# Router scores spread through memory, and the order of the loop's side stages changed, in a cross-attention and routed-FFN kernel

## The reference

```python
x = x + xattn(layernorm(x), ctx, mask)          # 16 heads of 16, 1024 keys, masked keys by column
x = x + routed_ffn(layernorm(x))
# routed_ffn, per batch of 512 rows y:
scores = y @ w_router
idx = top_k(scores, 128)                        # ordered by score, ties by position
x_sel = y[idx]; h = rmsnorm(x_sel, g1)
x_attn = causal_attention(h) @ W_out.T          # 128 rows, 16 heads
h2 = rmsnorm(x_sel + x_attn, g2)
x_ff = silu(h2 @ W1.T) * (h2 @ W2.T) @ W3.T
out = y.at[idx].set(x_sel + x_attn + x_ff)
```

## Time and profile before

| | |
|---|---|
| time, median of 3 runs | 895.89 us (893.83 to 895.96) |
| time of the profiled execution | 896.05 us |
| its span | 894.3 us |
| TensorE busy | 852.3 us, 95% of the span |
| ScalarE busy | 569.8 us, 64% |
| VectorE busy | 313.4 us, 35% |
| GpSimd busy | 123.5 us, 14% |
| mean granted TensorE clock | 0.993 of full speed |

### The profile page before, as it was taken

How to read it: one execution, slowest core, us unless ns; L and a number is a source line. 1 busy time by engine, 2 the same in 40 slices (tenths; PEclk the granted TensorE clock), 3 DMA queues, 4 the chain that set the end, 5 groups by cost and what they waited for, 6 DMA issues and landing times. The chain is left out here.

```text
span 894.3 us, 28250 instructions
## 1 busy us (share of the span) xinstructions
PE 852.3 (95%) x11779; PEld 294.9 (33%) x11785; DVE 313.4 (35%) x918; ACT 569.8 (64%) x644; POOL 123.5 (14%) x175
## 2 busy tenths in 40 slices
PE   7999999999999999999999999999999999989774
PEld 2322232324323332334323333234323342224343
DVE  3132135421552226421553316422354214411631
ACT  3566767676677767666577766676576766776110
POOL 4000102020120102120120101101121100210110
PEclk9999999999999999999999999999999999999898
DMA  5060201210011200111011200102001100200000
GB/s 183 17 227 1 78 3 31 55 58 24 7 37 49 79 8 27 59 32 49 9 37 49 79 8 25 45 20 78 7 10 53 31 8 2 61 1 4 7 25 9
DMA packets 27577, 35.56 MB, mean 40 GB/s; under 512 B 2083, under 2 KB 24142, under 8 KB 27448
## 3 DMA queue, kind: packets, MB, share of 16 engines
q1 hardware_dynamic: 24952, 31.73, 11.2%
q0 software_dynamic: 2496, 1.98, 1.4%
HBM read 27.53 MB, written 8.93 MB: 41 GB/s over the span
## 5 line engine op out<-in xcount | busy, mean ns | idle before, releaser
L511 ACT ACTIVATE probs<-pair_bank 128x1024 f32<-128x1024 f32 x512 | 496.3, 1021 | 225.4 <-ACTq L510 225.4
L481 PE MATMUL pair_bank<-q_sb,k_sb 32*64 32x512 f32 x4096 | 286.4, 612 | 10.0 <-PEq L478 9.6
L500 PE MATMUL o_bank<-probs,va 128*32 128x512 f32 x2048 | 273.3, 604 | 1.3 <-ACT probs L511 1.1
L500 PEld LDWEIGHTS o_bank<-probs,va 128*32 128x32 f32 x2048 | 41.5, 108 | 205.4 <-issue 114.2
L481 PEld LDWEIGHTS pair_bank<-q_sb,k_sb 32*64 32x64 f32 x4096 | 60.9, 129 | 145.0 <-issue 145.0
L266 PE MATMUL m_bank<-wv_sb,ctx_in 128*32 128x256 f32 x1024 | 61.5, 380 | 0.0
L266 PE MATMUL m_bank<-ctx_in,wk_sb 128*32 128x512 f32 x480 | 60.3, 592 | 0.0
L628 DVE TENSOR_SCALAR va<-m_bank,valid 128x256 f32<-128x256 f32 x64 | 28.1, 480 | 91.6 <-DVEq L625 91.6
L586 DVE STREAM_TRANSPOSE o_blk<-o_bank 128x512 f32<-128x512 f32 x32 | 22.9, 717 | 92.7 <-DVEq L585 92.7
L266 PEld LDWEIGHTS m_bank<-hid_t,w 128*32 128x32 f32 x1392 | 39.5, 110 | 17.0 <-issue 16.0
L266 PEld LDWEIGHTS m_bank<-wv_sb,ctx_in 128*32 128x32 f32 x1024 | 33.5, 110 | 34.2 <-issue 18.9
(11 more groups left out here) (173 smaller groups left out, 604.1 us busy)
## 6 DMA issues: line engine op xcount, KB each, us to landing
ctx_in<-in_ctxT SPq DMA_DIRECT2D x7, 1024.0 KB, 5.0
x_in<-in_x SPq DMA_DIRECT2D x8, 512.0 KB, 4.0
x<-in_x SPq DMA_DIRECT2D x8, 512.0 KB, 4.3
mask_in<-in_mask SPq DMA_DIRECT2D x8, 512.0 KB, 3.9
out_dram<-base SPq DMA_DIRECT2D x8, 512.0 KB, 5.5
ctx_in<-in_ctxT SPq DMA_DIRECT2D x2, 512.0 KB, 7.5
mask_row<-in_mask SPq DMA_DIRECT2D x8, 128.0 KB, 3.9
x_tok<-in_order SPq DMA_DIRECT2D x7, 128.5 KB, 2.0
```

The lines of the kernel that those rows point to most:

```text
L481: last = nc.tensor.matmul(pair_bank[pairs[r // 2]][j:j + 64, r % 2], key_tile(b, s, r)[:, j:j + 64], query_tile(b, s, r), start=True, stop ...
L500: last = nc.tensor.matmul(o_bank[32 * r:32 * r + 32], va[b % 2][:, t, HV * h:HV * h + 32], probs[s % 2][:, r], start=(t == 0), stop=(t == ...
L511: nc.scalar.activation(probs[s % 2][:, 2 * e:2 * e + 2, :], pair_bank[p][:], ACT.Exp, scale=HD ** -0.5).then_inc(s_free[p], 1)
```

## The change

Stage spread is gone from TensorE and ScalarE. SyncE now stores the scores to a DRAM row of 512 numbers, waits for that, and loads the row back to all 128 partitions. The row has the scores of rows 4p to 4p+3 of the (p t) layout side by side, so VectorE's order stages read it with a step of four numbers (16 bytes) where they read consecutive ones before; the second operand and the output are read and written as before. `pe_scores` waits for each pair of banks right before the two heads that go into it. In the loop's tables V0 moves from step 3 to step 0 (on VectorE it moves ahead of wo0), K00 as a whole becomes a stage of the batch two ahead, in steps 30 and 31, V1 is done in halves in steps 5 and 6 (on VectorE behind xn and ahead of order0), K01 moves up to steps 11 and 12 and Q1 down to 17 and 18, hidT and what follows it are one step earlier, and norm1 on VectorE stands behind k. Batch 0 does every P stage in halves over steps 8 to 29. The part "a"/"b" of `dve_norm` is not used by the tables.

```diff
-FS_STEP = 17
-PE_SLOT = [("P", "K00:1", 0, False), ("F", "wo0", 1, False), ("F", "wo1", 2, False), ("P", "V0", 3, True),
-           ("P", "K11:0", 4, False), ("P", "K11:1", 5, False), ("F", "spread", 6, False), ("P", "xT0", 7, False), ("P", "xT1", 8, False),
-           ("P", "Q0:0", 9, False), ("P", "Q0:1", 10, False), ("P", "V1", 11, False), ("P", "Q1:0", 12, False), ("P", "Q1:1", 13, False),
-           ("F", "hidT", 14, False), ("F", "q", 15, False), ("F", "k", 16, False), ("F", "v", FS_STEP, False),
...
-           ("F", "down:0", 29, False), ("F", "down:1", 30, False), ("X", "K00:0", 31, False)]
+FS_STEP = 16
+PE_SLOT = [("P", "V0", 0, False), ("F", "wo0", 1, False), ("F", "wo1", 2, False), ("P", "K11:0", 3, False), ("P", "K11:1", 4, False),
+           ("P", "V1:0", 5, False), ("P", "V1:1", 6, False), ("P", "xT0", 7, False), ("P", "xT1", 8, False), ("P", "Q0:0", 9, False),
+           ("P", "Q0:1", 10, False), ("P", "K01:0", 11, False), ("P", "K01:1", 12, False), ("F", "hidT", 13, False), ("F", "q", 14, False),
+           ("F", "k", 15, False), ("F", "v", FS_STEP, False), ("F", "fs", FS_STEP, False), ("P", "V2", FS_STEP, False),
+           ("P", "Q1:0", 17, False), ("P", "Q1:1", 18, False), ("F", "pv", 19, False), ("P", "V3", 20, False), ("F", "wout", 21, False),
...
+           ("F", "w1", 27, False), ("F", "down:0", 28, False), ("F", "down:1", 29, False), ("X", "K00:0", 30, False), ("X", "K00:1", 31, False)]
...
-DVE_ORDER = [("A", "norm3"), ("F", "wo0"), ("F", "wo1"), ("P", "V0"), ("F", "y"), ("P", "stats"), ("P", "xn"), ("F", "order0"),
-             ("F", "order1"), ("N", "norm0"), ("F", "order2"), ("F", "order3"), ("P", "Q0"), ("P", "V1"), ("F", "selected"), ("P", "Q1"),
-             ("F", "base"), ("F", "q"), ("N", "norm1"), ("F", "k"), ("P", "V2"), ("F", "pv"), ("P", "V3"), ("F", "wout"),
+DVE_ORDER = [("A", "norm3"), ("P", "V0"), ("F", "wo0"), ("F", "wo1"), ("F", "y"), ("P", "stats"), ("P", "xn"), ("P", "V1"), ("F", "order0"),
+             ("F", "order1"), ("N", "norm0"), ("F", "order2"), ("F", "order3"), ("P", "Q0"), ("F", "selected"), ("F", "base"),
+             ("F", "q"), ("F", "k"), ("N", "norm1"), ("P", "V2"), ("P", "Q1"), ("F", "pv"), ("P", "V3"), ("F", "wout"),
...
+        def spread_scores(sp):
+            sp.wait_ge(score_ready, 1)
+            sp.sem_inc(score_ready, -1)
+            sp.dma_start(score_row.rearrange("(p t) -> p t", t=QT), score[:]).then_inc(score_stored, 16)
+            sp.wait_ge(score_stored, 16)
+            sp.sem_inc(score_stored, -16)
+            sp.dma_start(all_scores[:], score_row.partition_broadcast(P)).then_inc(spread_in, 16)
...
             pairs = [ring(b, s, e) for e in range(2)]
-            for p in pairs:
-                pe.wait_ge(s_free[p], 1)
-                pe.sem_inc(s_free[p], -1)
             for r in range(HG):
+                if r % 2 == 0:
+                    pe.wait_ge(s_free[pairs[r // 2]], 1)
+                    pe.sem_inc(s_free[pairs[r // 2]], -1)
...
+                by_tile = lambda a: a.rearrange("p (t q) -> p t q", t=QT)
+                if note is put:
+                    others = all_scores[:].rearrange("p (q t) -> p t q", t=QT)
...
-                nc.vector.scalar_tensor_tensor(out=ties[0][:, ahead], in0=others[:, ahead], scalar=score[:, t:t + 1],
-                                               in1=before[:, t, ahead], op0=ALU.is_ge, op1=ALU.mult,
+                nc.vector.scalar_tensor_tensor(out=by_tile(ties[0][:])[:, ahead], in0=others[:, ahead], scalar=score[:, t:t + 1],
+                                               in1=by_tile(before[:, t])[:, ahead], op0=ALU.is_ge, op1=ALU.mult,
...
                 for b in range(B):
+                    if b > 0:
+                        spread_scores(sp)
                     if b + 2 < B:
                         load_x(sp, b + 2)
```

More of the change, by code:

```diff
@@ L67 @@
+ACT_SLOT = [("P", "K11", 4), ("P", "xT0", 7), ("P", "xT1", 8), ("P", "K01", 12), ("F", "hidT", 13), ("F", "v", FS_STEP),
+            ("F", "fs", FS_STEP), ("P", "differ", 20), ("P", "K10", 22), ("F", "hid2T", 23), ("F", "u0", 24), ("F", "u1", 26), ("X", "K00", 31)]
+DVE_ORDER = [("A", "norm3"), ("P", "V0"), ("F", "wo0"), ("F", "wo1"), ("F", "y"), ("P", "stats"), ("P", "xn"), ("P", "V1"), ("F", "order0"),
[2 rows of a table added]
              ("N", "norm2"), ("F", "u0"), ("F", "w0"), ("F", "u1"), ("F", "w1"), ("F", "down")]
@@ L69 @@
 PE_SLOT_0 = [("I", "V0", 0, False), ("I", "V1", 1, False), ("I", "K10", 2, False),
[4 rows of a table removed]
[L74 to L77, removed]
[7 rows of a table added]
@@ L78 @@
+ACT_SLOT_0 = [("I", "K10", 2), ("I", "K11", 4), ("P", "K00", 9), ("P", "K01", 11), ("P", "K10", 13), ("P", "K11", 15),
+              ("P", "xT0", 18), ("P", "differ", 20), ("P", "xT1", 21), ("X", "K00", 31)]
+DVE_ORDER_0 = [("I", "V0"), ("I", "V1"), ("I", "V2"), ("I", "V3"), ("I", "Q1"), ("P", "stats"), ("N", "norm0"), ("P", "xn"),
+               ("N", "norm1"), ("P", "V0"), ("P", "V1"), ("P", "V2"), ("N", "norm2"), ("P", "Q0"), ("P", "V3"), ("P", "Q1")]
 POOL_ORDER = [("F", "var"), ("P", "var"), ("F", "scatter"), ("F", "rms0"), ("F", "causal"), ("F", "rms1"), ("P", "differ"), ("F", "add")]
@@ L298, in pe_project @@
                 n = int(stage[1])
-                dst = take_bank(pe, i)
-                for e in range(2):
+                dst = bank[i] if part == 1 else take_bank(pe, i)
+                for e in share(part, 2):
                     t = 2 * n + e
@@ L303, in pe_project @@
                                    [(ctx_in[:, c, t * P:(t + 1) * P], wv[:, c, :]) for c in range(KC)])
-                last.then_inc(done["V"], 1)
+                if part != 0:
+                    last.then_inc(done["V"], 1)
             elif stage[0:2] == "xT":
@@ L713, in dve_ffn @@
                 note = put if stage[0:5] == "order" else select
[L715 to L725 removed]
+                by_tile = lambda a: a.rearrange("p (t q) -> p t q", t=QT)
+                if note is put:
+                    others = all_scores[:].rearrange("p (q t) -> p t q", t=QT)
+                    if t == 0:
+                        dve.wait_ge(spread_in, 16)
+                        dve.sem_inc(spread_in, -16)
+                elif i == MISC:
+                    others = by_tile(all_scores[:])
+                    if t == 0:
+                        dve.wait_ge(all_ready, 1)
+                        dve.sem_inc(all_ready, -1)
+                else:
+                    others = by_tile(bank[i])
+                    if t == 0:
+                        dve.wait_ge(done["spread"], 1)
+                        dve.sem_inc(done["spread"], -1)
+                ahead, behind = slice(0, t + 1), slice(t, QT)
+                nc.vector.scalar_tensor_tensor(out=by_tile(ties[0][:])[:, ahead], in0=others[:, ahead], scalar=score[:, t:t + 1],
+                                               in1=by_tile(before[:, t])[:, ahead], op0=ALU.is_ge, op1=ALU.mult,
                                                accum_out=rank[:, t, 0:1])
[L727 to L728 removed]
+                nc.vector.scalar_tensor_tensor(out=by_tile(ties[1][:])[:, behind], in0=others[:, behind], scalar=score[:, t:t + 1],
+                                               in1=by_tile(before[:, t])[:, behind], op0=ALU.is_gt, op1=ALU.is_gt,
                                                accum_out=rank[:, t, 1:2])
```

31 lines of the change are left out of this document (11 added, 20 removed), and 14 rows, old and new, of tables (PE_SLOT, PE_SLOT_0).

## The result

The changed kernel took 900.76 us in the median of 20 runs (896.77 to 903.44), the kernel before, beside it, 895.92 (893.38 to 898.64). The ratio is 1.005, 95% interval 1.0036 to 1.0064: 4.8 us slower, where + 5.6 was predicted. Its profiled execution took 897.49 us, near the low end of its own runs, with a span of 895.7.

What follows compares the result with a forecast made beforehand. TensorE, hardly ever idle in the loop, was taken to bound the kernel; - 3.9 - 3.5 - 3.4 + 4.9 + 0.9 + 7.2 + 3.4 = + 5.6 us gave 901.5 us, range 890.5 to 905.5.

Steps and rivals of the forecast that it cites:

- the likeliest case: The penalty of stepped reads on VectorE holds and hidT waits: 901.5 us, own range 897.5 to 906, chance 0.60.
- Batch 0: Of batch 0's 12 empty steps 11 get half a stage, each saving 0.36 us of waiting: 3.9 us less.
- Stage v: Step 17, batches 1 to 6: v's wait for a bank goes with k ahead of norm1 on VectorE, 3.4 us less.
- wo0 behind V0: Batches 1 to 6: wo0 waits for the bank VectorE's V0 frees behind norm3, 0.81 us each, 4.9 us more.
- xT0 behind V1: Batches 1 to 6: xT0 waits for the bank VectorE's V1 frees behind xn, 0.15 us each, 0.9 us more.
- The way of the scores: Store and load through memory take 5.0 us, bounds 4.2 and 8; order0 in batches 1 to 6 isn't delayed up to 6.6.
- Rival 3: The scores' round trip through memory is late, 8 us or more: 899.9 us, with the penalty near 911; chance 0.05.
- The step of 16 bytes: VectorE's order stages take 1.84 instead of 1.04 ns an element, making hidT wait 1.2 us a batch: 7.2 us more.
- Rival 2: Stepped reads cost VectorE nothing, hidT keeps its slot: 892.4 us, faster; chance 0.31.
- Batch 7: No side work covers the chain: hidT 1.6 us later, one more step behind it 2.1, less 0.3: 3.4 us more.
- Waits apart: Separate waits for the scores' bank pairs: worth 0.3 us behind hidT in batch 7, nothing in busy steps.
- Rival 4: Waiting apart breaks the scores up, a 0.05 us gap in each of 256 steps: 914 us, chance 0.02.

Runs made afterwards that it cites:

- the repeat: Both kernels run once more unchanged: before 895.46 us, changed kernel 898.74 us, ratio to before 1.0044, with profiled executions close to their medians.
- the first pair: The first measurement of both kernels with their profiled executions: changed kernel 900.76 us, kernel before 895.92 us, ratio 1.005.
- scores in tiles: Changed kernel plus a ScalarE copy that puts the transferred scores into tile order, so VectorE counts from unit steps: 900.33 us, ratio to before 1.0051.
- the new order without the transfers: Changed kernel, but scores spread as before by four transposes and a ScalarE copy, V1 whole in step 6: 894.7 us, ratio to before 0.9985.
- transfers alone: Kernel before with the scores spread by the two transfers and read with a step, stage spread removed, old order kept: 898.04 us, ratio 1.0027.

## Why the prediction was right

The direction, the size and the likeliest case held: + 5.6 predicted, + 4.8 and, in the repeat, + 3.3 measured. The mechanism is the predicted one: the stepped counts make hidT late in a slot without slack. But one of the prediction's own signs of being wrong did show: TensorE stood in two places that its list doesn't have, in step 12 of batch 0 and for 2.45 us at step 9 of batch 7. By its steps:

- **Batch 0**, - 3.9: measured - 2.3 and - 2.6 with K00:1 taken out. The steps are 2.90 us as said; the stall of 1.4 to 1.7 in step 12 is what is missing, and nothing in the trace of before told of it.
- **Spread**, - 3.5: held. Step 6 with its transposes (2.62) and V1 whole (3.77) became two steps of 2.90.
- **Stage v**, - 3.4: the wait went (step 17 was 6.44, and 6.79 in two batches; step 16 is 5.84), - 4.3. But the reason given, VectorE's order, was wrong by itself: k ahead in the old slots gives nothing. The step's words "it is covered as the k stage is a full step earlier than v" held for TensorE's bank and overlooked who stands behind k on VectorE, norm1, and who waits for that.
- **wo0 behind V0**, + 4.9: 0.57 in each batch (4.47 against 3.90; in batch 1 it was 4.12 already), + 3.2. The order on VectorE was as predicted (norm3 starts 1.24 behind the last values, 1.25 in the working), but behind norm3 the gap is 0.09 us (0.16), and the reads of the bank start 0.63 behind the copies (0.79): 5.32 in place of 5.57. The 0.5 a batch that moving the copies gave back shows that they are on the path.
- **xT0 behind V1**, + 0.9: steps of 2.63 to 2.94 instead of 2.63, + 0.7.
- **The way of the scores**, 5.0 us with bounds 4.2 and 8: the load's issue 1.48 behind the store's, 3.7 to its landing; in batch 7 VectorE was idle for 5.57 ahead of order0, and from the store's issue to the load's landing it took 5.05 to 5.93 over the batches. Rival 3 falls. By the Trainium skill's rule for the GpSimd path (DMA: Bandwidth & Descriptors, "Anatomy of one DMA") the pair was an estimated 4.6, 2.0 for the store and 2.6 for the load; this trace, with SyncE as the issuer, has 1.4 to 2.2 and 3.6 to 4.4.
- **The step of 16 bytes**, 1.84 ns for an element, + 0.5 in each order stage: in the mean of 14 counts each, 512 elements take 1.20 us and 128 take 0.47, so (1.20 - 0.47) / 384 = 1.9 ns, and an order stage takes 0.56 longer. The size was right, though its one source was a ScalarE row with another step. Rival 2 falls: the step was not free, 0.31 of the chance. Of what it does in batch 3, with S3 at 335.74: norm0 at S3 + 17.15 was predicted and 353.19 - 335.74 = 17.45 measured, so the values of step 9 are 0.25 late (+ 1.6 in all) where the sum had 0.05 of slack; hidT at S3 + 31.85 was predicted and 367.75 - 335.74 = 32.0 measured. It waits 1.08 there, and its step is 0.9 to 1.2 us longer over the batches, + 6.0 in the first pair and + 6.4 in the repeat against + 7.2. With unit steps in the new order this wait was gone in five of six batches, and the slack left was 0 to 0.5, about the 0.25 of the working.
- **Batch 7**, + 3.4: + 2.4 and + 3.2. HidT was predicted at S3 + 30.35 and came at + 31.1 and, in the repeat, + 30.6. The wait at step 9 of 2.45 and the clock behind it were not in the sum, nor was the wait of 2.39 at hidT in the repeat, behind which the clock fell too. Against that stood a stall of 1.5 us without a wait within step 17's scores in before, which the prediction named and left out, and which is not there in the changed kernel. That the sum came near is partly luck.
- **Waits apart**, nothing but 0.3: it is worth 2.5 us in the kernel before. In the changed kernel batch 0 has one empty step left, so little of that can remain; no run takes it out there. Rival 4 falls.

The sum for batches 1 to 6 was + 6.1 and came to + 3.3: - 0.9 from v, - 1.7 from wo0, - 1.2 from hidT, + 1.6 from step 9, and - 0.2 each from xT0 and from V0's own step; two tenths are left. With batch 0, 1.3 to 1.6 above its term, errors of both signs cancel in part, so the nearness of + 5.6 to + 4.8 owes something to luck.

The change as a whole, taken apart by ratios: the waits apart - 2.5 us, batch 0 in halves - 2.5 (not independent), the new order with both - 1.3, the way through memory + 5. In the old order the same way through memory costs 2.4, and nothing in batches 1 to 6: it is the two together, stepped counts and a slot without slack, that cost most. The new order by itself adds nothing to the two good parts: it spends on wo0 (+ 3.2) most of what it gains at v (- 4.3), and loses in batch 7. The version to keep is the kernel before with the waits apart, with or without batch 0 in halves. The new order with transposes and with V0's copies behind its reads might reach some 3 us below its 894.7, an estimate from the 0.5 us of each step 1; that wasn't run.

## What to carry to other kernels

When a stage is moved one slot earlier, work out the slack of everything that feeds it, down to how an operand lies in memory. Here the old slot had 3.5 us of slack in batches 1 to 6 and the new one 0.5 or less. In the old slot 0.56 us more in each of four counts cost nothing, and neither did a load that landed a microsecond late; in the new one the counts cost 6 us. When two works on an in-order engine are swapped, follow both: who waits for the one now behind matters as much as who was waiting for the one now ahead. An isolated experiment on each part showed that the part with the least text, a wait taken half a group later, was worth as much as all the rest.

## What the runs showed of the hardware

- VectorE takes 1.9 ns an element from a row read every fourth float32 (1.20 us for 512 elements, 0.47 for 128, in the mean), against 1.04 for consecutive ones. ScalarE is no better: a copy of 128x512 with a step of 16 bytes takes 1.12 us where the step is on the writing side and 1.17 where it is on the reading side, instead of 0.60. The Trainium skill (SBUF — State Buffer, "Door 1: The DMA port swizzle") speaks of lines of 16 bytes; by these rows a step of exactly one line is not free on either engine.
- From the issue of a store of 2 KB to memory to that of the load that waits for it took 1.5 to 2.3 us with pieces of 16 bytes, and 8.3 to 10.4 with pieces of 4 bytes.
- TensorE's granted clock fell to the lower level (1.2 GHz) right behind a standstill in the loop: after 2.45 us (after), 3.17 (scores in tiles), 2.97 (the new order without the transfers) and 1.57 (transfers alone) of idle time the same groups took 1.7 to 2.0 us instead of 1.1, for 4 to 7 us. Behind the waits of 1.08 us in batches 1 to 6 it did not fall, nor behind 1.80 at hidT in batch 7 of the changed kernel, so the length of the standstill alone does not decide.
- The kernel before took 895.5 us on two chips and 905.5 on a third. Two programs with its tables have a trace from the third: in one VectorE starts 1.8 us instead of 0.2 behind the matmuls that it waits for, at the same place in six batches, in the other it doesn't. What decides is not shown.
